# A recurrence kernel: the reciprocal moves from ScalarE's logarithm and exponential, with a Newton step, to VectorE's own operation

## The reference, cut to what matters

```python
def step(carry, kv_t):                 # one time step, for each sequence and channel
    p, q, o = carry
    kt, vt = kv_t
    no = jnp.maximum(o, u + kt)
    A, E = jnp.exp(o - no), jnp.exp(u + kt - no)
    y = (A * p + E * vt) / (A * q + E)  # the quotient this case is about
    no2 = jnp.maximum(w + o, kt)
    A2, E2 = jnp.exp(w + o - no2), jnp.exp(kt - no2)
    return ((A2 * p + E2 * vt, A2 * q + E2, no2), y)

x = x + wkv(w, u, layernorm(x), ctx)     # the recurrence, 128 steps
x = x + ffn(layernorm(x))                # 2 shared experts (512 -> 2048 -> 512, gelu), 16 routed ones, top 2
```

## Time and profile before

| | |
|---|---|
| median of 3 runs | 921.85 us (920.21 to 922.37) |
| the profiled execution: its time, its span | 922.2 us, 920.6 us |
| TensorE busy | 849.9 us (92%) |
| VectorE busy | 647.8 us (70%), 1345 instructions |
| ScalarE busy | 485.3 us (53%), 859 instructions |
| granted TensorE clock, mean | 0.995 |

### The profile page before, as it was taken

One profiled execution on the slowest core, in us unless ns is written; L12 is line 12 of the kernel. 1 busy time (PEld: TensorE's weight loads), 2 busy tenths in 40 slices (PEclk: granted clock), 3 DMA queues, 4 the chain that ended last, 5 costly groups with the idle time before them and its releaser, 6 DMA issues.

```text
span 920.6 us, 14811 instructions
## 1 busy us (share of the span) xinstructions
PE 849.9 (92%) x4018; PEld 695.8 (76%) x4018; DVE 647.8 (70%) x1345; ACT 485.3 (53%) x859; POOL 179.5 (19%) x223
## 2 busy tenths in 40 slices
PE   0198999999999999999999999999999899999997
PEld 0166878888788888887888888878888777777885
DVE  7985899856577778565777785645775777773774
ACT  5433866445366553453666534435553566775541
POOL 2000000012100000121000001210212666653660
PEclk9999999999999999999999999999999999999999
DMA  9144434458453333582533335655794466667885
GB/s 220 49 144 138 116 115 115 118 117 178 69 161 92 97 109 95 125 172 66 160 96 108 96 103 103 87 188 161 152 232 120 141 209 211 213 192 261 290 252 169
DMA packets 125855, 134.40 MB, mean 146 GB/s; under 512 B 10256, under 2 KB 87616, under 8 KB 125276
## 3 DMA queue, kind: packets, MB, share of 16 engines
q1 hardware_dynamic: 116844, 108.47, 44.5%
q0 software_dynamic: 8784, 25.11, 9.2%
q10 hardware_dynamic: 160, 0.02, 0.0%
HBM read 110.58 MB, written 22.98 MB: 145 GB/s over the span
## 4 chain that ended last, share of the span: by engine, by line
PE 91%; DVE 3%; issue 2%; DMA 2%; ACT 1%; SPq 1%; POOLq 0%; POOL 0%; DVEq 0%; ACTq 0%
PE up L561 13%; PE up L563 12%; PE up L562 12%; PE acc L604 12%; PE acc L609 12%; PE acc L606 12%; PE up L761 4%; PE up L763 2%; PE acc L561 2%; PE up L665 1%; PE acc L563 1%; PE acc L562 1%; PE misc L748 1%; PE up L748 1%; PE acc L674 1%
## 5 line engine op out<-in xcount | busy, mean ns | idle before, releaser
L561 PE MATMUL up<-xs,w1hi 128*128 128x512 f32 (+1 forms) x512 | 200.1, 391 | 5.3 <-ACT xs L896 4.6
L562 PE MATMUL up<-xs,w1hi 128*128 128x512 f32 (+1 forms) x512 | 196.5, 384 | 0.0
L563 PE MATMUL up<-xs,w1lo 128*128 128x512 f32 (+1 forms) x512 | 196.5, 384 | 0.0
L604 PE MATMUL acc<-w2hi,hhi 128*128 128x512 f32 x490 | 190.8, 389 | 1.3 <-issue 1.3
L606 PE MATMUL acc<-w2lo,hhi 128*128 128x512 f32 x490 | 190.7, 389 | 0.0
L834 ACT ACTIVATE hhi<-up,b_col 128x512 fp32r<-128x512 f32 (+1 forms) x128 | 86.8, 678 | 150.1 <-PE up L563 125.3
L1053 DVE TENSOR_TENSOR hlo<-hf,hhi 128x512 fp32r<-128x512 f32 (+1 forms) x128 | 86.0, 672 | 88.8 <-ACT hf L837 56.3
L609 PE MATMUL acc<-w2hi,hlo 128*128 128x512 f32 x490 | 131.7, 389 | 0.0
L561 PEld LDWEIGHTS up<-xs,w1hi 128*128 128x128 f32 x512 | 96.2, 188 | 24.9 <-ACT xs L896 5.2
L563 PEld LDWEIGHTS up<-xs,w1lo 128*128 128x128 f32 x512 | 96.2, 188 | 19.4
L562 PEld LDWEIGHTS up<-xs,w1hi 128*128 128x128 f32 x512 | 96.3, 188 | 18.3 <-issue 0.2
(11 more groups left out here) (243 smaller groups left out, 1135.8 us busy)
## 6 DMA issues: line engine op xcount, KB each, us to landing
w_raw<-in_L_ffn_sw SPq DMA_DIRECT2D x270, 256.0 KB, 3.1
expert_rows<-ysb SPq DMA_DIRECT2D x47, 256.0 KB, 2.5
vin<-in_ctx SPq DMA_DIRECT2D x16, 256.0 KB, 8.4
xn_rows<-kn POOLq DMA_DIRECT2D x16, 256.0 KB, 8.0
e2raw<-in_L_ffn_ew SPq DMA_DIRECT2D x16, 256.0 KB, 5.1
ew_sb<-in_L_ffn_ew SPq DMA_DIRECT2D x16, 256.0 KB, 7.0
X<-in_x SPq DMA_DIRECT2D x12, 256.0 KB, 9.9
out<-X SPq DMA_DIRECT2D x12, 256.0 KB, 4.6
```

The costliest lines, as they stand in the source:

```text
L561: nc.tensor.matmul(o, lhs[0], rhs[0], start=start, stop=False)
L562: nc.tensor.matmul(o, lhs[0], rhs[1], start=False, stop=False)
L563: return nc.tensor.matmul(o, lhs[1], rhs[0], start=False, stop=stop)
L604: nc.tensor.matmul(acc[t][:], hh, w2hi[:, slot], start=first and (q > 0 or t >= HT) or again, stop=False)
```

## The change

VectorE's part 7 gets its reciprocal from one instruction of its own, and one product follows. ScalarE's `wkv_reciprocal` goes, with its two functions a round and the table loads that it called for. The waits that stood in it (for `den`, and for the transpose back of the round before, which reads `yy`) go to VectorE.

```diff
-            def wkv_reciprocal(r):
-                act.wait_ge(wkv.sem, wkv.at(r, "den"))
-                if not isinstance(r, int) or r:
-                    act.wait_ge(wkv.sem, wkv.at(r - 1, "ty"))
-                nc.scalar.activation(yy[:], den[:], ACT.Ln).then_inc(wexp.sem, 1)
-                act.wait_ge(wexp.sem, wexp.at(r, "ln"))
-                nc.scalar.activation(yy[:], yy[:], ACT.Exp, scale=-1.0).then_inc(wexp.sem, 1)
...
-            wkv_reciprocal(0)
             wkv_exp(1)
...
-            for p in range(4):
+            for p in range(5):
                 pre_gelu(p)
-            nc.scalar.preload_act_table_set("natural_log_exp_and_others")
-            wkv_reciprocal(1)
-            pre_gelu(4)
...
-                    if j == 6:
-                        nc.scalar.preload_act_table_set("natural_log_exp_and_others")
-                        wkv_reciprocal(r)
...
                 elif part == 7:
-                    after(wexp, r, "rec")
-                    do(V.tensor_tensor(den[:], den[:], yy[:], ALU.mult))
-                    after(wkv, r, "nt")
-                    do(V.scalar_tensor_tensor(out=yy[:], in0=den[:], scalar=-2.0, in1=yy[:],
-                                              op0=ALU.add, op1=ALU.mult))
-                    after(wkv, r, "nr")
-                    do(V.scalar_tensor_tensor(out=yy[:], in0=yy[:], scalar=-1.0, in1=num[:],
-                                              op0=ALU.mult, op1=ALU.mult))
+                    after(wkv, r, "den")
+                    if not first:
+                        after(wkv, r - 1, "ty")
+                    do(V.reciprocal(yy[:], den[:]))
+                    after(wkv, r, "rec")
+                    do(V.tensor_tensor(yy[:], yy[:], num[:], ALU.mult))
```

More of the change, by code:

```diff
@@ L292, in mixed_layer @@
         wt = Steps(sem("wt"), "tk tv")
-        wkv = Steps(sem("wkv"), "es ev h hv cq cp sp sq den num nt nr y ty")
-        wexp = Steps(sem("wexp"), "e ln rec")
+        wkv = Steps(sem("wkv"), "es ev h hv cq cp sp sq den num rec y ty")
+        wexp = Steps(sem("wexp"), "e")
         ln2 = Steps(sem("ln2"), "s0 s1 s2 s3 a0 a1 a2 a3 veps")
```

## The result

The changed kernel takes 930.53 us (median of 4 runs, 929.73 to 931.36) where the kernel before takes 922.11 (4 runs); the ratio is 1.0093, with a 95% interval of 1.0073 to 1.0113. It is slower by about 8.4 us. The profiled execution has a span of 928.1 us, 7.5 more than before. What follows accounts for these 7.5 us; the missing 0.9 lies between this one execution, the fastest of the four, and the median.

The account below looks back on a forecast made before the run. VectorE's time was taken to bound the kernel only where TensorE waits for it, at the start and for `w2lo` in the loop. The terms, 6.1 + 1.3 + 4.3 + 2.0 + 1.2 = 14.9 us, gave 936.8 us; range 924 to 942.

Parts of the forecast that it names:

- the two places: Where TensorE waits for VectorE: the start, for the norm's halves, and the loop, for `w2lo`; only there would the change count.
- R: Time of VectorE's one RECIPROCAL over 1024 elements, taken as 8.6 us, with bounds 1.2 and 9.4.
- rival two: The reciprocal takes about 6.6 us (5 to 7.5), so the kernel is +7.0, 928.9 us; chance 0.22.
- the case that I gave 0.52: The main case: a reciprocal of 7.5 to 9.5 us, so a kernel time of 931 to 942 us.
- Reading (b): Price of the reciprocal with its fixed cost from wider rows: 7.3 or 6.3 ns an element, 6.6 us over 1024.
- Round 0, +6.1: At the start, the quotient takes 9.86 us instead of 3.74, and all 6.1 us of it delay the kernel.
- Round 1, +1.3: Late half of the start: another 4.56 us, of which VectorE's 3.03 us idle before `w1hi` covers most; +1.3 us.
- Chunk 10, +4.3: After round 2's quotient, `w2lo` comes 4.6 us later, less 0.31 already lost: TensorE waits +4.3 us more.
- Clock, +1.2: TensorE's granted clock falls after a stall of 4 us at chunk 10: +1.2 us, bounds 0 and 2.
- Rounds 3, 5 and 7, +2.0: Second round of later blocks: `w2lo`'s lead at chunks 20, 52, 84 overdrawn by 0.35, 0.6, 1.0 us; +2.0 in all.
- Rival four: The relief of ScalarE, 35 us, is what counts; at most a further 1 to 2 us gained; chance 0.02.
- The signs: Expected in the profile: reciprocal row near 8600 ns, later transposes, waits at chunk 10 and three later chunks, 14 fewer table loads.

Follow-up runs that it names:

- the kernel with halves: The changed kernel with round 2's reciprocal in two instructions of 512 elements, after chunks 8 and 9; ratio 1.0075 to the kernel before.
- rounds 0 and 1: The kernel before with VectorE's reciprocal in rounds 0 and 1 only, the old way elsewhere; ratio 1.0044 to the kernel before.
- round 0 alone: The kernel before with VectorE's reciprocal in the first round only; ratio 1.0039 to the kernel before.
- ScalarE's part kept: The changed kernel with ScalarE's logarithm, exponential and table loads kept, their result overwritten by VectorE's reciprocal; ratio 1.0141 to the kernel before.
- the doubled one: The changed kernel with the reciprocal worked twice, to the same result, in rounds 4 and 6; ratio 1.0169 to the kernel before.
- rounds 3 to 7: The kernel before with VectorE's reciprocal in these rounds only, cut into pieces in rounds 5 to 7; ratio 0.9987 to the kernel before.
- The mixed kernel: The kernel before with VectorE's reciprocal in rounds 3 to 7 (round 7 in pieces) and no Newton step in round 0; 919.07 us against 921.80.

## Why the prediction was right, and where a size was off

The sign, the two places and the mechanism were right; R was too large, and with it the sum: 936.8 forecast, 930.5 measured, near rival two (R = 6.6, 928.9). So the case that I gave 0.52 (R of 7.5 to 9.5, 931 to 942) did not come, and rival two, which I gave 0.22, did; the range held because it took in both.

- **R, the term that was mis-sized.** 8.6 us forecast, 6.54 measured. It came from one 178 ns row over 4 elements less a one-element row's 145, times 256. A difference of 33 ns cannot carry that: the same instruction on 4 elements takes 158 in another place, and below 16 elements the time isn't linear. Reading (b), with a fixed cost taken from wider rows, came to 6.6 and was right in number, but by luck: its fixed cost of 152 ns is not the 93 of the large sizes, and its own numbers give (178 - 152) / 4 = 6.5 ns and R = 6.8; the 6.3 that it took instead was an allowance without a row. The trace stands between the two rates that the prediction drew from the Trainium skill: with the 0.96 GHz of "VectorE: DVE Perf Modes", section "Specifications", 6.30 ns are, as an estimate, 6.0 cycles an element, neither 8 nor one. Neither page states a rate: 8 cycles was my reading of the first one's repeat count, and "in one pass", so one element a cycle, my reading of the second one's chain of divides.
- **Round 0, +6.1.** With the measured R it is +4.06, and the trace shows it whole on the early norm: +3.61 with x 0.46 earlier.
- **Round 1, +1.3.** I had the cover of 3.03 us move with the early half one to one. With R = 6.54 this would leave 0. In the changed kernel's profiled execution `w1hi` came only 1.8 us later (69.60 to 71.41), since its transfer landed 3.2 us after its issue instead of 5.0, and the late norm ended up bound by VectorE alone: 6.1 us later at its statistics, less 3.2 of idle time, +2.8. So the start as a whole lost less than round 0 did, 2.87 for 4.06. That was this execution's luck with a transfer, and no fault of the working: in the kernel with halves, which has the same start, `w1hi` came 3.98 us later than before (73.58) and the late norm's transposes too (76.39), which is the forecast's one to one. The runs of rounds 0 and 1 and of round 0 alone confirm that round 1 adds little; what sets the time of that transfer was not tried.
- **Chunk 10, +4.3.** By the same working with the measured R, 4.06 - 1.49 - 0.31 = 2.26; measured 2.38. The kernel with ScalarE's part kept shows the 1.49 by itself, and the doubled one shows that the lead predicts a gap to 0.1 us.
- **Clock, +1.2.** Measured 1.57, as the offset's growth behind the gap. The prediction took for granted that a gap of this kind costs clock; at chunk 74 of the doubled kernel one cost 0.12.
- **The sum with the measured R.** By the same working it is 4.06 + 0 + 2.26 + 0 + 1.2 = 7.5, and the trace has 7.5. That they agree is partly luck: the start gave 1.19 less than 4.06, and the clock, chunk 28 and the last stage about as much more.
- **Rounds 3, 5 and 7, +2.0.** Nothing, as R was smaller: the leads fell to 1.6, 1.4 and 1.4 where the working with the measured R gives 4.06 - 2.4 = 1.7 for the first and 1.1 to 1.5 for the others. With the lateness of the kernel that keeps ScalarE's part they are overdrawn, as forecast.
- **Rival four**, ScalarE's relief, fell as a gain: rounds 3 to 7 free ScalarE and gain nothing beyond 0.2%. The prediction was wrong that no wait of TensorE in the loop names ScalarE: three do, for `xs`, 1.45, 1.57 and 1.57 us as the next block is taken up. They are the same in the changed kernel, so nothing hung on it. As cover for a late VectorE it counts, which the prediction had at chunk 9 and, too small, in round 1.
- The 0.37 near chunk 28 and the 0.3 in the last stage have no cause that a run shows. The kernels with halves and with the doubled cost don't have the 0.37, so it is no steady cost of the change.
- **The signs.** The early and late transposes came at 45.37 and 75.18 us for 47.9 and 79.8; VectorE's wait for the exponential went and 14 table loads with it (36 to 22), as said; the three short waits behind rounds 3, 5 and 7 did not come.

## What to carry to other kernels

An engine's load share says little about an edit; the lead of what it makes over its use, chunk by chunk, says almost all: 4.06 us more of VectorE's time cost nothing where the lead was 3.5 us or more, and 2.4 us, besides the clock, where the lead was 0.1 and an idle time of 1.49 stood before. Don't scale an operation's price up from a row of a few elements: 20 ns of uncertainty in the fixed cost of a 4-element row were 5 us over 1024 elements, so such a price needs a wide range. One trace is one sample of the start, which varied by 1.1 us here between kernels that start in the same way: small differences there want many executions. The mixed kernel is 0.3% faster than before, but by a step of the computation that it leaves out in round 0; the best version with the whole computation (rounds 3 to 7, 0.9987) is ahead by less than the 0.2% that can be told here.

## What the runs showed of the hardware that was not expected

- VectorE's RECIPROCAL costs 6.30 ns an element in float32 from 16 to 1024 elements, about 6 times the 1.04 ns of a TENSOR_TENSOR's (684 ns over 512 elements, 1215 over 1024), with a smaller constant: 93 ns, where the same two rows of TENSOR_TENSOR leave 153. Cut into eight pieces it took 6.63 us in all, for 6.55 in one.
- GpSimd's product over 1024 elements (2.35 us) stretched VectorE's from 1.18 to 2.81 us while they ran side by side. By the two records they overlapped for 1.74 us, and VectorE lost 2.81 - 1.18 = 1.63 of it: an estimate from one instruction (and GpSimd's spans are rough), by which it all but stood still. The trace agrees with the Trainium skill, "GPSIMD Engine Reference", section "1. Specifications", by which the two engines share their way to SBUF and collide when VectorE's instruction has two SBUF inputs.
- Two gaps of TensorE of the same length, 2.63 us, in one kernel: the granted clock was 0.67 over the 4 us behind one and 1.00 behind the other. The gap of 2.52 in the changed kernel cost 1.57 us more by the clock, the two of 0.30 and 1.98 in the kernel with halves the same 1.57, and the one of 4.24 with ScalarE's part kept 2.45. At the start, a wait of 4.37 was followed by a clock of 0.57 over 4 us, one of 3.41 in the changed kernel by 0.58, and one of 3.89 between them by 1.00. So the length of the gap alone does not decide it; what does stays open.
